# Attention's unnormalised sums moved by SyncE transfers to a feature-major array, divided once per eight heads

## What is computed

```python
def _L0_attn_ref(x, w_qkv, w_out):
    ...
    logits = jnp.einsum('bhsd,bhtd->bhst', q, k) * scale
    mask = jnp.tril(jnp.ones((S, S), dtype=bool))
    logits = jnp.where(mask, logits, neg_inf)
    probs = jax.nn.softmax(logits, axis=-1)
    probs = probs * mask.astype(probs.dtype)
    out = jnp.einsum('bhst,bhtd->bhsd', probs, v)
    out = out.transpose(0, 2, 1, 3).reshape(B, S, D_MODEL)
    return jnp.einsum('bsi,oi->bso', out, w_out)

x = x + 0.5 * _L0_ffn_ref(_layernorm(x, axis=-1), ...)
x = x + _L0_attn_ref(_layernorm(x, axis=-1), L0_attn_w_qkv, L0_attn_w_out)
x = x + 0.5 * _L0_ffn_ref(_layernorm(x, axis=-1), ...)
```

## Time and profile before

| | |
|---|---|
| median of 3 runs | 2117.75 us (2114.55 to 2118.36) |
| the profiled execution | 2126.23 us |
| its span, first to last instruction | 2124.5 us |
| attention, from the first scores to the last "pv" | 368 to 1794 us |
| busy over the span: PE, DVE, ACT, POOL | 96%, 86%, 75%, 20% |
| mean granted TensorE clock | 0.975 of full speed |

### The profile page before, as it was taken

The page is one execution under the profiler, slowest core; times in us unless marked ns, Lnnn a source line. Parts: engine busy times, 40 slices in busy tenths (PEclk is TensorE's granted clock), DMA queues, the critical chain, the costliest instruction groups (busy, mean ns, idle before and its releaser), DMA issues.

```text
span 2124.5 us, 99858 instructions
## 1 busy us (share of the span) xinstructions
PE 2047.7 (96%) x43659; PEld 1584.0 (75%) x43659; DVE 1817.7 (86%) x4023; ACT 1598.6 (75%) x3311; POOL 414.5 (20%) x1118
## 2 busy tenths in 40 slices
PE   5899989999999999999999999999999999879998
PEld 3788866377877777777787777777778776658885
DVE  6666666899999999999999999999999994676665
ACT  5344446599999999999999999999999998334442
POOL 1333213411121111121111111111111111023330
PEclk8899989999999999999999999999999999979998
DMA  8211103300010000100001001000010002231112
GB/s 273 74 47 50 42 16 125 134 30 25 13 34 14 25 30 8 34 20 18 31 7 33 22 16 34 9 29 27 11 34 16 22 4 69 54 118 47 45 49 88
DMA packets 70394, 94.36 MB, mean 44 GB/s; under 512 B 16640, under 2 KB 59396, under 8 KB 69956
## 3 DMA queue, kind: packets, MB, share of 16 engines
q1 hardware_dynamic: 62796, 68.75, 10.1%
q0 software_dynamic: 6816, 19.20, 3.4%
q10 hardware_dynamic: 344, 0.01, 0.0%
HBM read 62.24 MB, written 25.43 MB: 41 GB/s over the span
## 4 chain that ended last, share of the span: by engine, by line
PE 88%; DVE 6%; issue 2%; ACT 1%; POOL 1%; DMA 1%; SPq 1%; another core or an unknown queue 0%; DVEq 0%; ACTq 0%; POOLq 0%
PE bank L1264 39%; PE bank L1257 22%; PE bank L1139 17%; PE bank L1346 3%; PE bank L1150 1%; PE bank L1375 1%; DVE stats L1405 1%; PE bank L1307 1%; PE bank L1157 1%; DVE rows L1427 1%; DVE x_res L1725 1%; SPq L698 0%; POOL work L591 0%; DVE work L1594 0%; PE bank L1217 0%
## 5 line engine op out<-in xcount | busy, mean ns | idle before, releaser
L966 ACT ACTIVATE feat<-bank 128x512 f32<-128x512 f32 (+3 forms) x2304 | 1263.2, 565 | 113.8 <-PE bank L1264 13.3
L1264 PE MATMUL bank<-work 96*32 96x512 bf16 (+2 forms) x15872 | 1206.4, 370 | 5.0 <-DVE work L1772 3.8
L1772 DVE TENSOR_REDUCE work<-bank 128x1 f32<-128x512 f32 (+1 forms) x1920 | 1178.9, 659 | 26.4 <-PE bank L1264 23.4
L1257 PE MATMUL bank<-feat,phase 128*17 128x128 f32 (+3 forms) x18432 | 879.2, 263 | 0.3 <-ACT feat L972 0.3
L1257 PEld LDWEIGHTS bank<-feat,phase 128*17 128x17 f32 x18432 | 588.4, 98 | 270.7 <-ACT feat L972 13.7
L1264 PEld LDWEIGHTS bank<-work 96*32 96x32 bf16 (+1 forms) x15872 | 472.6, 96 | 57.1 <-DVE work L1772 24.6
L1139 PE MATMUL bank<-work 128*128 128x256 f32 (+1 forms) x1872 | 398.4, 363 | 0.6 <-issue 0.2
L1139 PEld LDWEIGHTS bank<-work 128*128 128x128 f32 x1872 | 325.1, 192 | 37.1 <-issue 1.0
L625 POOL TENSOR_SCALAR_AFFINE_SELECT feat<-feat 128x128 f32<-128x128 f32 x512 | 145.1, 292 | 456.0 <-ACT feat L966 439.1
L1656 DVE COPY work<-phase 128x514 f32 x234 | 101.5, 436 | 124.1 <-ACT work L880 99.5
L578 POOL DMA_INDIRECT work<-token_table,row_no x142 | 138.1, 973 | 299.0 <-PE bank L1150 142.6
(11 more groups left out here) (201 smaller groups left out, 1371.9 us busy)
## 6 DMA issues: line engine op xcount, KB each, us to landing
phase<-in_w SPq DMA_DIRECT2D x12, 1024.0 KB, 12.0
work<-qk_parts SPq DMA_DIRECT2D x60, 192.0 KB
token_table<-rows SPq DMA_DIRECT2D x8, 1056.0 KB, 8.7
work<-work SPq DMA_DIRECT2D x512, 0.5 KB
qk_parts<-phase SPq DMA_DIRECT2D x20, 384.0 KB, 2.8
work<-qk_parts SPq DMA_DIRECT2D x60, 128.0 KB
qk_parts<-work SPq DMA_DIRECT2D x12, 384.0 KB, 2.8
x_res<-in_x SPq DMA_DIRECT2D x8, 512.0 KB
```

Of the source, the lines that this page charges most:

```text
L966: eng.activation(p_ring[:, n % P_RING, lo:QB], s_bank("probs", n)[:, lo:QB], ACT.Exp, scale=HD ** -0.5).then_inc(sig.s_done, 1)
L1257: mm = eng.matmul(bank[ACC_BANK][GRID * g:GRID * g + VW, GRID * i0:P], v_aug[:, t, h, :], weights[:, i0:TPJ, g, :], start=(t == 0), stop=( ...
L1264: mm = eng.matmul(out[GRID * g:GRID * (g + 1), width], left[:, GRID * g:GRID * (g + 1)], right, start=start, stop=stop)
L1772: eng.tensor_reduce(maxima[:, h % 2, j, PLACE[i], at:at + 1], scores[:, 0:hi - lo], AX_X, ALU.max).then_inc(sig.a_done, 1)
```

## The change

Five things are changed together.

- "turn" is gone, and so are `sums` and the small `recip`. In place of the turn SyncE issues eight transfers per unit in its step "acc": four copy the sums of a group (16 partitions x 128 numbers) to the head's 16 rows of a feature-major array `heads` in `rows`, and four copy the group's total, one row of 128 numbers, to 16 rows (`totals_of`). ScalarE may write `acc_out` again once the eight transfers of the unit two before have landed (`moved`).
- "divide" is a step of VectorE alone and is there for the last head of each eight: 16 times in all, for heads 7 and 15 and each j. It waits for the transfers, takes the reciprocal of 128 x 512 totals in place and multiplies 128 x 512 sums. It stands 8 items after the unit's "acc" (`DIVIDE_LAG`), the last one after all items.
- TensorE's transpositions of the heads and ScalarE's copies of them are gone: the output projection reads `heads` as it lies and waits for the division of the 512 tokens concerned.
- What is in `rows` or `work` has changed places for the second feed-forward: normalised rows go to `work` (`rows_of`), the widened ids and one-hots to `rows` (`hcarve(f, n)`).
- The second load of the expert weights waits for all 16 divisions as well, and the first staging of the second feed-forward for the stored table.

```diff
-PV_LAG, PV_PAUSE, TURN_LAG, DIVIDE_LAG = 5, 1, 2, 2
+PV_LAG, PV_PAUSE, DIVIDE_LAG = 5, 1, 8
...
             if t == TPJ * (j + 1) - 1:
                 yield "acc", h * NJ + j
-                unturned.append((n + TURN_LAG, h * NJ + j))
+                if h % HEADS_PER_PART == HEADS_PER_PART - 1:
+                    undivided.append((n + DIVIDE_LAG, h * NJ + j))
...
-                    elif what == "divide":
-                        h, j = UNITS[n]
-                        need.wait_ge(sig.recip, n + 1)
-                        eng.tensor_tensor(heads[:, TPJ * j:TPJ * (j + 1), h * HD:(h + 1) * HD], sums[:, n % 2, :, 0:HD],
-                                          bc(recip[:, n % 2, :], 2, [P, TPJ, HD]), ALU.mult).then_inc(sig.divided, 1)
...
                 if f == 1:
                     need.wait_ge(sig.pv, PV_ALL)
+                    need.wait_ge(sig.divided, KD * NJ)
...
+                elif what == "acc":
+                    h, j = UNITS[n]
+                    need.wait_ge(sig.acc, n + 1)
+                    if h >= HEADS_PER_PART:
+                        need.wait_ge(sig.divided, divisions(h - HEADS_PER_PART, j))
+                    at = h % HEADS_PER_PART * HD
+                    for g in range(TPJ):
+                        summed = summed_of(h, j)[at:at + HD, :].rearrange("p (i g b) -> p i g b", i=TPJ, g=TPJ)
+                        eng.dma_start(summed[:, :, g, :],
+                                      acc_out[GRID * g:GRID * g + HD, n % 2, :].rearrange("p (i b) -> p i b", i=TPJ)
+                                      ).then_inc(sig.moved[n % 2], 16)
+                        eng.dma_start(totals_of(h, j)[at:at + HD, g * P:(g + 1) * P],
+                                      bc(acc_out[GRID * g + HD:GRID * g + VW, n % 2, :], 1, [1, HD, P])
+                                      ).then_inc(sig.moved[n % 2], 16)
...
                         need.wait_ge(sig.pv, pv_at[unit_end(h, j)])
-                        need.wait_ge(sig.turned, n - 1)
+                        need.wait_ge(sig.moved[n % 2], 16 * MOVES * (n // 2))
                         eng.activation(acc_out[:, n % 2, :], bank[ACC_BANK][:, 0:P], ACT.Copy).then_inc(sig.acc, 1)
...
-            def transpose_heads(n):
-                need.wait_ge(sig.a_done, len(A_ITEMS))
-                need.wait_ge(sig.divided, len(UNITS))
...
+                for i2 in range(g * LN_GRP[2], (g + 1) * LN_GRP[2], 2):
+                    need.wait_ge(sig.divided, divisions(H - 1, i2 // TPJ))
+                    need.wait_ge(sig.a_done, len(A_ITEMS))
+                    need.wait_ge(sig.acc, len(UNITS))
+                    need.wait_ge(sig.attended, i2 // 2 - 1)
+                    bk = 4 + i2 // 2 % 2
+                    for i in (i2, i2 + 1):
+                        for k in range(KD):
+                            eng.matmul(bank[bk][:, (i - i2) * D:(i - i2 + 1) * D], heads[:, k, i * P:(i + 1) * P],
+                                       w_out_sb[:, k, :], start=(k == 0),
+                                       stop=(k == KD - 1)).then_inc(sig.out_mm, 1)
...
-                    elif what == "turn":
-                        need.wait_ge(sig.acc, n + 1)
-                        need.wait_ge(sig.divided, n - 1)
-                        eng.transpose(sums[:, n % 2].rearrange("p i w -> p (i w)"),
-                                      acc_out[:, n % 2, :]).then_inc(sig.turned, 1)
                     elif what == "divide":
-                        need.wait_ge(sig.turned, n + 1)
-                        need.wait_ge(sig.divided, n - 1)
-                        eng.reciprocal(recip[:, n % 2, :], sums[:, n % 2, :, HD]).then_inc(sig.recip, 1)
+                        h, j = UNITS[n]
+                        need.wait_ge(sig.moved[n % 2], 16 * MOVES * (n // 2 + 1))
+                        summed = summed_of(h, j).rearrange("p (i g b) -> p i g b", i=TPJ, g=TPJ)
+                        totals = totals_of(h, j).rearrange("p (g i b) -> p i g b", i=TPJ, g=TPJ)
+                        eng.reciprocal(totals_of(h, j), totals_of(h, j)).then_inc(sig.recip, 1)
+                        need.wait_ge(sig.recip, divisions(h, j))
+                        eng.tensor_tensor(summed, summed, totals, ALU.mult).then_inc(sig.divided, 1)
```

113 lines of the change are left out of this document (42 added, 71 removed).

## The result

| | before | after |
|---|---|---|
| median of 4 runs each, one chip | 2118.06 us (2114.55 to 2118.85) | 2337.95 us (2334.15 to 2340.35) |
| span of the profiled execution | 2124.5 us | 2336.5 us |
| mean granted TensorE clock | 0.975 | 0.940 |
| attention, first to last copy of an accumulator | 1378.8 us | 1593.9 us |
| from the last copy to the span's end | 330.2 us | 331.7 us |

The ratio is 1.104 (95% interval 1.103 to 1.105). The forecast was 2188 us with a range of 2150 to 2228: the sign was right, the size was wrong by 150 us. All of it lies in attention, which takes 215.2 us more; ahead of it the profiled execution of after was 4.6 us quicker, and behind it 1.5 us slower.

The account below looks back on a forecast made before the run. TensorE was taken to set the pace, VectorE following closely. Relief -5, stops 62.7, clock 12 and the end 1 made +71 us on the profiled execution; the median of 2117.75 plus 70.5 gave 2188 us, range 2150 to 2228.

Parts of the forecast that it names:

- The relief (-5 us): Attention: removing VectorE's turn and small reciprocal takes away 5 us of TensorE's waits, with ends 0 and 12.
- The price of a reciprocal: VectorE's divisions: a 128x512 reciprocal takes 4.3 us, extrapolated from 4 and 8 elements; with the multiplication 5.0 us.
- the three bounds: Guesses for one 128x512 reciprocal: 4.4 us by slope, 2.2 us between, 0.69 us at the low end; 4.3 taken.
- the cheap rivals: Cheaper reciprocals: 2.2 us giving 2152 us (0.08), 0.69 us giving 2124 (0.04), under 1.7 us giving 2101 (0.07).
- the 70 us of the sum: Heads 7 and 15: 14 divisions in the way of score reductions, each stopping VectorE 5.0 us.
- What the banks hold back (-12.7 us): Heads 7 and 15: TensorE runs ahead by three banks, so it does not feel 12.7 us of VectorE's stops.
- the clock (+12): Heads 7 and 15: TensorE's granted clock falls behind 14 stops, 0.85 us each, 12 us, ends 0 and 24.
- 62.7: Heads 7 and 15: the stops' total in us, 70 of divisions plus 5.4 of waits minus 12.7 held by banks.
- Waits of divisions for their transfers: Heads 7 and 15: VectorE waits 5.4 us for landings, ends 0 and 25; 0.5 us an issue, 1.25 landing.
- SyncE's queue: Attention: eight issues per unit put 4 us before the maxima at unit 4 only; costs nothing, end 10 us.
- the queue is the bound: Rival: issues over 0.72 us stop ScalarE's copy, and TensorE, at every head's second unit; 2226 us, chance 0.11.
- The end of attention: Last division, projection and first statistics behind attention: statistics 1.5 us later; +1 us taken, ends -3 and +4.

Follow-up runs that it names:

- divisions only: The changed kernel without its 1024 transfers, dividing a block of ones at the same places, waiting only for the copy; 2188.7 us, 1.029 of before.
- pieces of 1.24 us: Changed kernel with totals' transfers on GpSimd, four copy buffers, divisions 16 items late, each cut into four pieces three items apart; 2197.4 us, 1.039 of before.
- the head of 92 us: A head of 92.2 us in the changed kernel with the four totals' transfers of each unit issued by GpSimd instead of SyncE; 2221.0 us, 1.045 of before.
- this arrangement: The changed kernel with totals' transfers on GpSimd, four buffers for the copied accumulator, divisions 16 items behind their copy; 2200.5 us, 1.040 of before.

## Why the prediction was wrong, step by step

**The relief (-5 us): none.** In "divisions only" the ordinary heads have neither the turn nor the small reciprocal and keep 86.7 us. The waits of the earlier trace rows that I charged to VectorE did not go with its work.

**The price of a reciprocal: 3.35 us, not 4.3.** The slope from 4 to 8 elements, 8.3 ns, was too steep; from 128 to 512 elements it is (3352 - 943)/384 = 6.3 ns. The choice between the three bounds was right, and none of the cheap rivals came near. With 4.04 us a stop, the 70 us of the sum become 57 for 14 stops.

**What the banks hold back (-12.7 us) and the clock (+12): together not -0.7, but +4.** The 14 divisions cost 60.4 us and are 56.6 us long. How the two terms share that is not settled. TensorE's idle time grew by only 39.6 us, which speaks for banks that hold back as much as forecast or more; its busy time grew by 20.8, which speaks for a clock term above 12 and within its end of 24. But a busy TensorE is not TensorE at its peak, and the granted clocks of heads 7, 8 and 15 (0.91, 0.98, 0.93) make at most 20 us. By them the banks held back between nothing and 16 us. The slow stretch of 3.4 us that the clock term counted is too short: in the earlier trace rows it makes (0.38 + 0.47) x 4 / 0.5 = 6.8 us, and behind the stop in after it lasted as long. That VectorE has a tenth of its time to spare (ten reads in 5.86 us) is doubtful: pieces of 1.24 us, each about as long as what I thought the banks lend, cost nearly as much as whole divisions, and the earlier trace rows has VectorE idle for 6.85 of 400 us, 1.5 us in a head.

**For the divisions the errors cancel.** 62.7 + 12 - 5 = 70 was forecast for everything in attention, with the reciprocal too dear by 13; the divisions alone measure 61. That this half came near is partly luck.

**Waits of divisions for their transfers: 30.5 us, not 5.4**, beyond the end of 25. An issue took not 0.5 but 0.73 us of the queue and a landing 2.3, not 1.25 us. The 1.25 came from the maxima, transfers of 8 rows of 64 bytes; the new ones are 8 KB over 16 partitions. It was also misread: rows 8 show when bytes move, and not when the semaphore tells of them. Where TensorE waits for such a transfer, it is 1.59 us from issue to landing (838.24 above). The Trainium skill's fixed 2.0 us ("DMA: Bandwidth & Descriptors", section "Anatomy of one DMA"), which I gave beside it and did not take, was nearer to the 2.3 measured.

**SyncE's queue: 0, with an end of 10 us. This is the step that failed.** It measured 117 us in the ordinary heads, 4 in head 0, and presumably some 9 each in heads 7 and 15, where it cannot be told from the divisions' waits. I compared the eight issues of one unit with the room in front of one row of maxima, 4 us against 3 to 4, and stopped there. But around a head's start four units end within 15 us, each with its eight, and a queue keeps what it could not do. The sum over those units, 32 x 0.5 = 16 us with my own price and 32 x 0.73 = 23 with the measured one, beside maxima and parts, was never made. The rival "the queue is the bound" had the right culprit and the wrong test: it looked at ScalarE's copy in unit 1 (1.5 us, when it came), put the threshold at 0.72 us for a single issue, and priced only that wait, 38 us of what became 160.

**The end of attention: +1 us, measured +1.5**, though not as described: the last division starts 6.7 us after the copy, not 4.75, and the first statistics come 17.3 us behind it, where before it was 13.4; 4 us more, of which later stages give back most.

```profile
2011.54 3.35 DVE L1784 RECIPROCAL feat<-feat 128x512 f32<-128x512 f32 x1 [10.49 <-DMA feat<-feat]
2014.93 0.69 DVE L1786 TENSOR_TENSOR rows<-rows,feat 128x512 f32<-128x512 f32 x1
...
2022.16 2.70 DVE L1397 BATCH_NORM_STATS2 stats<-x_res 128x6 f32<-128x256 f32 x8
```

**Open.** Why GpSimd stands for 3 us between two blocks of issues in the head of 92 us, what holds the head of 89, and 7 or more of the 22 us that this arrangement costs beside the divisions. How much the banks hold back. Why one issue in eight lasts over 1 us.
